# Gated attention loop: the chunk's small jobs between its two value products, the second maxima behind them, and two 8-column steps with other operands

## The chip, the cores and the metric

The kernel runs on one core of a Trainium2 chip as a single program. The metric is the device time of one execution in microseconds; the number compared is the median of several runs.

## The reference

Four layers follow each other on `x` of shape (2, 1024, 128), each as `x = x + layer(layernorm(x))`: a linear ("flow") attention layer with feed-forward part, a gated attention layer, a narrow multi-head attention layer, and a mixture of experts. The change lies in the second, which is:

```python
s = sigmoid(x @ Ws)                                   # (b, t, 8 heads)
vals, idx = top_k(s, 3)
scores = zeros_like(s).at[bi, ti, idx].set(vals)      # gates: 3 of 8 heads
q, k, v = heads(x @ Wq), heads(x @ Wkv)               # 8 heads of 64
attn = softmax(einsum('bhid,bhjd->bhij', q * 64**-0.5, k))
out = einsum('bhij,bhjd->bhid', attn, v)
proj = einsum('bhtd,hde->bhte', out, Wo) + bo
return einsum('bhte,bth->bte', proj, scores)
```

## The kernel before, in words

The gated phase works on 8 pairs of heads (2 batches of 4 pairs, `G = 2` heads in a pair), each in two halves of 512 query columns. These are `HALVES = 16` halves `n`. For each half the 1024 keys are 8 tiles of 128, taken in `CHUNKS = 4` chunks `c` of two tiles, so that the loop has 64 chunks. "Chunk (n, c)" names one. The loop stands once in the program of each engine; semaphores join them, and no engine reorders its own list.

In each chunk TensorE makes the scores of two key tiles into PSUM banks 0 to 3 (`score`, L1453 for the negative shift and L1460 for the products). ScalarE takes the exponential (`probs`, L1567). TensorE multiplies the probabilities of the chunk before with the values (`mix`, L1473, twice in a chunk, into bank 4), and GpSimd adds them up (`tally`, L1327, two instructions in most chunks) for the denominators.

The softmax needs the row maxima of a half before its scores. They are made far ahead, as "pairs": two score products (`maximum`, L1355) whose results VectorE reduces (L1671, into `maxima`). Eight pairs make a half, and two pairs go into a chunk, the first and the second maxima. After the last pair of a half VectorE merges two columns of maxima into `top` (L1676, 128x8), TensorE turns it in the job `shift` (L1368), VectorE writes `shift_t` (L1690), and SyncE carries it to the row `neg`.

Everything else is a small "job":

- `proj`: projection of a later pair of heads (L71 to L73). ScalarE copies it to `high` (L1516), VectorE subtracts to `low` (L1662).
- `den`: denominators of the half before, from `tally` (L1373); VectorE copies them to `den_rows` (L1694).
- `dent`: those rows turned back (L1378). VectorE inverts eight columns into `inv` (L1701) and multiplies them by the gates into `coef` (L1704).
- `out`, for each of the two heads: the output product (L1408, both in one stretch); VectorE adds it to `X` with `coef` (L1730, four instructions a head).
- `turn`, `bias` (halves 2 to 5, chunks 0 and 1), `gate` and its choice (half 0), and the jobs `fturn`, `fproj`, `fvalue` that prepare the next phase (halves 10 to 13; L1036, L71 to L73, L1713, L1717, L1720).

All jobs and maxima share three PSUM banks, 5 to 7, in rotation: `order` is the list of all of them, `number` a job's place in it, `bank_of(job) = JOB_BANK + number[job] % 3`. TensorE may write a bank once VectorE has used the job three places before, which it learns from the counter `job_used`. A pair waits `job_used >= number[pair[1]] - 2`, an output product `job_used >= number - 1` of its first job. VectorE walks through `order` strictly.

`between(n, c)` lists the jobs that stand behind the first maxima: in order `shift` (c = 2), `proj` (chunks 0 and 1 of even halves, 2 and 3 of odd ones), `gate`, `fturn`, `fproj`, `fvalue`, then `den` (c = 2) or `dent` (c = 3). `behind(n, c)` lists the output products (c = 3) and `turn` and `bias`. TensorE's order in a chunk is: scores, first maxima, first value product, `between`, second maxima, second value product, `behind`.

From chunk (14, 2) on there are no maxima any more. The loop ends with `den`, `dent` and `out` of the last half, and a barrier leads to the narrow attention phase.

Of the kernel before, what the change touches and what calls it, by code (L numbers as in the profile page):

```python
# [13 lines left out]
ALU = mybir.AluOpType  # L14
ACT = mybir.ActivationFunctionType
AX = mybir.AxisListType
# [4 lines left out]
P = 128  # L21
# [941 lines left out]
class Front:  # L963
# [5 lines left out]
    H, DH, G = 16, 8, 4  # L969
# [146 lines left out]
def gated_attention_phase(nc, psum, X, C, io, stale, front):  # L1116
# [5 lines left out]
    H, DH, TOPK, G = 8, 64, 3, 2  # L1122
# [5 lines left out]
    QT = BANK // P  # L1128
    STEPS = G * QT
# [5 lines left out]
    with ExitStack() as ctx:  # L1135
        ph = Phase(nc, ctx, "gated")
# [38 lines left out]
        front_U = old_values[:, PARTS:PARTS + SEQ].rearrange("p (t d) -> p t d", d=D)  # L1175
        front_UH, front_UL = UH[:, 0:SEQ], UL[:, 0:SEQ]
        front_rest = w_raw[:, 0:2 * BANK].rearrange("p (k t) -> p k t", k=2)
        inv = ph.sb("inv", [P, STEPS])
        coef = ph.sb("coef", [P, 2, STEPS])
        norm = Norm(ph, "norm", X, U)  # L1180
        shift_ready, ws_zero = ph.sem("shift_ready"), ph.sem("ws_zero")
# [58 lines left out]
        def behind(n, c):  # L1240

            now = []
            if n >= 1 and c == 3:
                now += [("out", n - 1, 0), ("out", n - 1, 1)]
            if 2 <= n < 2 + QUARTERS and c < 2:
                now.append((("turn", "bias")[c], n - 2))
            return now

        def maxima_of(n, c, e):
            i = n_lead + 2 * (n * CHUNKS + c) + e  # L1250
            return max_pair(i) if i < HALVES * MAXPAIRS else []

        tail = [("den", HALVES - 1), ("dent", HALVES - 1), ("out", HALVES - 1, 0), ("out", HALVES - 1, 1)]
        order = lead + [job for n in range(HALVES) for c in range(CHUNKS)
                        for job in maxima_of(n, c, 0) + between(n, c) + maxima_of(n, c, 1) + behind(n, c)] + tail
        number = {job: i for i, job in enumerate(order)}

        def bank_of(job):
# [73 lines left out]
        def _(pe):  # L1332
# [163 lines left out]
            for n in range(HALVES):  # L1496
                for c in range(CHUNKS):
                    i = n * CHUNKS + c
                    score(n, c)
                    for e in range(2):  # L1500
                        pair = maxima_of(n, c, e)
                        if pair:
                            maximum(pair)
                        if i >= 1:
                            mix(i - 1, e)
                        small((between, behind)[e](n, c))
            for e in range(2):
                mix(HALVES * CHUNKS - 1, e)
            small(tail)
# [81 lines left out]
        def _(dve):  # L1591
# [51 lines left out]
            for i, job in enumerate(order):  # L1643
                bank = bank_of(job)
                if job in position:
                    here = position[job]
                    if here in STATS_AT:
                        dve.wait_ge(job_used, number[("out", 6 + STATS_AT[here], 1)] + 1)
                        front.norm.quarter_stats(dve, STATS_AT[here])
                    if here == CENTER_AT:  # L1650
                        for q in range(PERB):
                            front.center(dve, q)
                    if here in LOWEST_AT:
                        front.lowest(dve, LOWEST_AT[here], front_part, front_rest)
                if job in (max_pair(6)[0], max_pair(8)[0]):
                    turned_low(2 + (job == max_pair(8)[0]))
                if job[0] == "proj":
                    _, g, m, x = job
                    parts += 1
                    cols = slice(x * BANK, (x + 1) * BANK)  # L1660
                    dve.wait_ge(high_taken, parts)
                    dve.tensor_tensor(low[:, g % 3, m, cols], psum[:, bank, :], f32(high[:, g % 3, m, cols]),  # L1662
                                      ALU.subtract).then_inc(job_used, 1)
                    continue
                dve.wait_ge(job_done, i + 1)
                if job[0] == "max":
                    _, n, j, qt, x = job
                    if n >= 2 and j == qt == x == 0:
                        dve.wait_ge(top_ready, n - 1)
                    at = j * QT + qt  # L1670
                    dve.tensor_reduce(maxima[:, n % 2, x, at:at + 1], psum[:, bank, :], AX.X, ALU.max).then_inc(job_used, 1)  # L1671
                    if (j, qt, x) == (G - 1, QT - 1, 1):
                        dve.wait_ge(job_used, i + 1)
                        if n >= 1:
                            dve.wait_ge(job_done, number[("shift", n - 1)] + 1)
                        dve.tensor_tensor(top[:, :], maxima[:, n % 2, 0, :], maxima[:, n % 2, 1, :], ALU.max).then_inc(top_ready, 1)  # L1676
                    if job in CHOICE_AT:
                        choose_step(CHOICE_AT[job])
                elif job[0] == "gate":
                    turned_gates = psum[:, bank, :].rearrange("p (i q s) -> p q i s", q=QUARTERS, s=32)[:, :, :, 0:H]  # L1680
                    by_quarter = scores[:, :, :].rearrange("p (q i) h -> p q i h", q=QUARTERS)
                    dve.tensor_scalar(by_quarter, turned_gates, 1.0, None, ALU.add).then_inc(gate_step, 1)
                    dve.wait_ge(gate_step, 1)
                    dve.reciprocal(scores[:, :, :], scores[:, :, :]).then_inc(gate_step, 1)
                    dve.sem_inc(job_used, 1)
                elif job[0] == "shift":
                    n = job[1]
                    if n >= 1:
                        dve.wait_ge(shift_loaded, 64 * n)
                    dve.tensor_scalar(shift_t[:, :], psum[0:STEPS, bank, 0:P], -1.0, None, ALU.mult).then_inc(job_used, 1)  # L1690
                    dve.wait_ge(job_used, i + 1)
                    dve.sem_inc(shift_copied, 1)
                elif job[0] == "den":
                    dve.tensor_copy(den_rows[:, :], psum[:, bank, :]).then_inc(job_used, 1)  # L1694
                elif job[0] == "dent":
                    n = job[1]
                    t0, h0 = n // 2 // PAIRS * STILES + n % 2 * QT, n // 2 % PAIRS * G
                    dve.wait_ge(job_used, i)
                    if n == 0:
                        dve.wait_ge(gate_step, 8)  # L1700
                    dve.reciprocal(inv[:, :].rearrange("p (t j) -> p t j", j=G),  # L1701
                                   psum[:, bank, :].rearrange("p (t j d) -> p t j d", j=G, d=DH)[:, :, :, 0]).then_inc(inv_ready, 1)
                    dve.wait_ge(inv_ready, n + 1)
                    dve.tensor_tensor(coef[:, n % 2, :].rearrange("p (t j) -> p t j", j=G), inv[:, :].rearrange("p (t j) -> p t j", j=G),  # L1704
                                      gates[:, t0:t0 + QT, h0:h0 + G], ALU.mult).then_inc(job_used, 1)
                elif job[0] == "turn":
                    if job[1] >= 1:
                        dve.wait_ge(job_done, number[("bias", job[1] - 1)] + 1)
                    dve.tensor_copy(gates_t[:, :], psum[0:H, bank, :]).then_inc(job_used, 1)
                elif job[0] == "fturn":  # L1710
                    front.turned_low(dve, bank, job[1], front_UH, front_UL)
                    dve.wait_ge(front.lo_turned, job[1] + 1)
                    dve.sem_inc(job_used, 1)  # L1713
                elif job[0] == "fproj":
                    front.without_high(dve, bank, job[1], front_part, front_rest)
                    dve.wait_ge(front.rest_ready, job[1] + 1)
                    dve.sem_inc(job_used, 1)  # L1717
                elif job[0] == "fvalue":
                    to, made = front.value_view(bank, job[1])
                    dve.tensor_copy(to, made).then_inc(job_used, 1)  # L1720
                elif job[0] == "bias":
                    dve.wait_ge(job_used, i)
                    part = X[:, job[1] * PER_Q:(job[1] + 1) * PER_Q, :]
                    dve.tensor_tensor(part, part, psum[:, bank, :].rearrange("p (t d) -> p t d", d=D), ALU.add).then_inc(job_used, 1)
                else:
                    _, n, j = job
                    t0 = n // 2 // PAIRS * STILES + n % 2 * QT
                    dve.wait_ge(job_used, i)
                    for t in range(QT):
                        last = dve.scalar_tensor_tensor(X[:, t0 + t, :], psum[:, bank, tile(t)],  # L1730
                                                        coef[:, n % 2, t * G + j:t * G + j + 1], X[:, t0 + t, :], ALU.mult, ALU.add)
                    last.then_inc(job_used, 1)
# [710 lines left out]
```

## Time and profile before

| | |
|---|---|
| median of 3 runs | 1275.22 us |
| lowest and highest run | 1272.82, 1278.53 us |
| profiled execution, its own time | 1267.5 us |
| its span, first to last instruction | 1265.7 us |
| gated loop, scores of (0, 0) to the last update of `X` | about 208 to 623.6 us |
| mean granted clock of TensorE | 0.934 |

The span lies inside the execution's own time. Everything that is worked out from the trace belongs to the profiled execution, so it is set against 1267.5 us and not against the median. A row of a timeline has the start, the duration (for merged instructions until the last one ends), the engine, the line, what it writes and reads, how many instructions it holds, and in brackets how long the engine was idle before it and for whom. Matmuls overlap their successors, so the time between the starts of two rows says what one costs in a busy stretch.

### The profile page before, as it was taken

To read this page: it belongs to the slowest core of one execution; us is meant where nothing else is said; L and a number is where in the kernel's file an instruction comes from. 1 tells how busy PE (TensorE), PEld (TensorE's weight loads), DVE (VectorE), ACT (ScalarE), POOL (GpSimd) and SP (SyncE) were. 2 spreads that over 40 slices of the span, in tenths; PEclk is the share of its full clock that TensorE was granted. 3 is DMA by queue.
4 is the path that set the end of the run, shared out by engine and by line. 5 is a ranking of instruction groups with operands and counts; after the bars stand their busy time and mean duration, and the time that the engine had idled before them with its cause. 6 is when DMAs were issued, how large, how long until landed. Compare 5 with 4: busy or idle time off the path is not lost. (4 is left out here: it accounts for less than half of the span.)

```text
span 1265.7 us, 18746 instructions
## 1 busy us (share of the span) xinstructions
PE 1106.5 (87%) x6921; PEld 558.3 (44%) x6921; DVE 951.1 (75%) x1606; ACT 712.1 (56%) x1207; POOL 377.9 (30%) x239
## 2 busy tenths in 40 slices
PE   4389959999999989999789999999999778999995
PEld 3256735444444444444232222222222276888884
DVE  7958488767666766675589999999998176778777
ACT  5224546333333354433327777878787727888883
POOL 1038212755767656667500000000000021112110
PEclk9569979989999999999859999999999968999998
DMA  3000010000000000001020000000000023143421
GB/s 90 1 1 3 1 34 2 10 1 1 1 2 2 2 1 1 26 18 35 15 73 18 16 24 15 26 13 27 13 2 1 1 35 77 43 84 62 76 47 33
DMA packets 46354, 29.43 MB, mean 23 GB/s; under 512 B 10992, under 2 KB 43000, under 8 KB 46264
## 3 DMA queue, kind: packets, MB, share of 16 engines
q1 hardware_dynamic: 46264, 28.24, 9.5%
q8 instruction: 55, 0.90, 0.3%
q14 instruction: 35, 0.29, 0.1%
HBM read 23.57 MB, written 4.26 MB: 22 GB/s over the span
## 5 line engine op out<-in xcount | busy, mean ns | idle before, releaser
L2032 DVE TENSOR_REDUCE narrow_att_maxima<-psum 128x1 f32<-128x1024 f32 x256 | 301.8, 1219 | 28.6 <-PE psum L1884 26.0
L1991 ACT ACTIVATE narrow_att_probs<-psum 128x512 f32<-128x512 f32 x512 | 266.4, 603 | 79.2 <-PE psum L1910 79.1
L1327 POOL TENSOR_TENSOR gated_tally<-gated_probs,gated_tally 128x1024 f32<-128x1024 f32 x96 | 230.1, 2397 | 72.5 <-ACT gated_probs L1567 64.0
L1567 ACT ACTIVATE gated_probs<-psum 128x1024 f32<-128x1024 f32 x128 | 124.3, 1022 | 202.3 <-PE psum L1460 202.3
L1671 DVE TENSOR_REDUCE gated_maxima<-psum 128x1 f32<-128x512 f32 x256 | 164.3, 683 | 59.2 <-PE psum L1355 57.3
L1910 PE MATMUL psum<-narrow_att_q,narrow_att_k 50*128 50x512 bf16 x448 | 145.4, 383 | 6.3 <-ACT narrow_att_probs L1991 5.2
L1923 PE MATMUL psum<-narrow_att_probs,narrow_att_v_ones 128*32 128x512 f32 x1024 | 137.2, 607 | 10.3 <-ACT narrow_att_sums L1981 10.2
L1884 PE MATMUL psum<-narrow_att_k,narrow_att_q 48*128 48x512 bf16 x448 | 130.3, 380 | 16.3 <-DVE narrow_att_maxima L2032 11.7
L1473 PE MATMUL psum<-gated_probs,gated_values 128*64 128x512 f32 x512 | 138.0, 619 | 0.0
L2324 DVE TENSOR_TENSOR moe_hidden_lo<-moe_hidden,moe_hidden_hi 128x512 fp32r<-128x512 f32 x144 | 100.8, 725 | 46.8 <-ACT moe_hidden_hi L2293 46.4
L2289 ACT ACTIVATE moe_hidden<-psum,moe_up_bias 128x512 f32<-128x512 f32 x144 | 96.0, 685 | 37.1 <-PE psum L73 35.9
L1884 PEld LDWEIGHTS psum<-narrow_att_k,narrow_att_q 48*128 48x128 bf16 x448 | 27.0, 94 | 137.5 <-DVE narrow_att_maxima L2032 126.1
L2293 ACT ACTIVATE moe_hidden_hi<-moe_hidden 128x512 fp32r<-128x512 f32 x144 | 86.4, 628 | 0.0
L1355 PE MATMUL psum<-gated_high 64*128 64x512 f32 x256 | 58.6, 452 | 17.5 <-DVE gated_low L1662 10.4
L1327 POOL TENSOR_TENSOR gated_tally<-gated_probs 128x1024 f32<-128x1024 f32 x16 | 37.9, 2372 | 89.7 <-ACT gated_probs L1567 89.7
L1910 PEld LDWEIGHTS psum<-narrow_att_q,narrow_att_k 50*128 50x128 bf16 x448 | 32.9, 93 | 58.2 <-ACT narrow_att_probs L1991 53.9
L1460 PE MATMUL psum<-gated_high 64*128 64x512 f32 x256 | 58.4, 451 | 0.0
L71 PE MATMUL psum<-moe_UH,moe_up_hi 128*128 128x512 f32 x144 | 58.3, 405 | 0.0
L72 PE MATMUL psum<-moe_UL,moe_up_hi 128*128 128x512 f32 x144 | 58.1, 404 | 0.0
L73 PE MATMUL psum<-moe_UH,moe_up_lo 128*128 128x512 f32 x144 | 57.6, 400 | 0.0
L71 PE MATMUL psum<-moe_hidden_hi,moe_down_hi 128*128 128x512 f32 x144 | 57.1, 396 | 0.0
L72 PE MATMUL psum<-moe_hidden_lo,moe_down_hi 128*128 128x512 f32 x144 | 57.0, 396 | 0.0
(362 smaller groups left out, 1836.5 us busy)
## 6 DMA issues: line engine op xcount, KB each, us to landing
moe_mixb<-moe_mix_scratch SPq DMA_DIRECT2D x8, 1024.0 KB, 15.9
moe_raw_up<-in_L_ffn_up_w SPq DMA_DIRECT2D x8, 256.0 KB, 16.1
moe_raw_down<-in_L_ffn_down_w SPq DMA_DIRECT2D x8, 256.0 KB, 12.1
narrow_parts_scratch<-gated_values SPq DMA_DIRECT2D x12, 128.0 KB, 2.1
narrow_parts_scratch<-narrow_att_part SPq DMA_DIRECT2D x12, 128.0 KB, 2.1
narrow_att_q<-narrow_parts_scratch SPq DMA_DIRECT2D x14, 96.0 KB
narrow_att_q<-narrow_parts_scratch SPq DMA_DIRECT2D x42, 32.0 KB
narrow_att_k<-narrow_parts_scratch SPq DMA_DIRECT2D x14, 96.0 KB
```

The lines of the kernel that those rows point to most:

```text
L71: pe.matmul(out, a_hi, b_hi, start=start, stop=False, skip_group_check=True)
L72: pe.matmul(out, a_hi, b_lo, start=False, stop=False, skip_group_check=True)
L1327: pool.tensor_tensor(tally[:, n % 2, :, :], probs[:, kt % 4, :, :], so_far, ALU.add).then_inc(tallied, 1)
L1473: last = pe.matmul(psum[DH * j:DH * j + DH, SUM_BANK, :], values[:, t, c0:c0 + DH], probs[:, kt % 4, j, :], start=(kt == 0), stop=(kt == S ...
L1567: act.activation(probs[:, k % 4, :, :], psum[:, 2 * e:2 * e + 2, :], ACT.Exp, scale=SCALE).then_inc(exped, 1)
L1671: dve.tensor_reduce(maxima[:, n % 2, x, at:at + 1], psum[:, bank, :], AX.X, ALU.max).then_inc(job_used, 1)
L1884: done = pe.matmul(psum[:, i % 2 * 2 + x, :], qs(n // 2, n % 2, r)[64 * a:64 * a + ROWS, tile(qt)], ks(n // 2, x, r)[64 * a:64 * a + ROWS, ...
L1910: pe.matmul(psum[:, SCORE_BANK + j % 3, :], ks(n // 2, kt // QT, e)[rows, tile(kt % QT)], qs(n // 2, n % 2, e)[rows, :], start=True, stop= ...
L1923: last = pe.matmul(psum[32 * j:32 * j + 32, SUM_BANK, :], v_ones[:, n // 2 % 2, kt, j, :], probs[:, (n * STILES + kt) % 3, j, :], start=(k ...
L1991: act.activation(probs[:, k % 3, 2 * e + u % 2, :], psum[:, SCORE_BANK + j % 3, :], ACT.Exp, scale=SCALE).then_inc(exped, 1)
L2032: dve.tensor_reduce(maxima[:, n % 2, column(u):column(u) + 1], chunk.rearrange("p a b -> p (a b)"), AX.X, ALU.max).then_inc(chunk_used, 1)
L2324: dve.tensor_tensor(hidden_lo[:, k % 2, a, :], hidden[:, k % 2, a, :], f32(hidden_hi[:, k % 2, a, :]), ALU.subtract).then_inc(hidden_lo_re ...
```

## The change

Three edits, all in the gated phase:

1. The order in a chunk, for all engines and on TensorE. It becomes: scores, first maxima, first value product, `between`, `behind`, second value product, second maxima. The numbers of the jobs change with it, and so the banks and waits.
2. The inverse of the denominators is written back to the PSUM columns that it was read from, `inv` is gone, and `coef` is made from `gates` in SBUF and those columns in PSUM.
3. `top` is made by one reduction over the two columns of maxima instead of an element-wise maximum of two SBUF operands.

```diff
-        inv = ph.sb("inv", [P, STEPS])
...
-                        for job in maxima_of(n, c, 0) + between(n, c) + maxima_of(n, c, 1) + behind(n, c)] + tail
+                        for job in maxima_of(n, c, 0) + between(n, c) + behind(n, c) + maxima_of(n, c, 1)] + tail
...
                     for e in range(2):
+                        if i >= 1 and e == 1:
+                            mix(i - 1, 1)
                         pair = maxima_of(n, c, e)
                         if pair:
                             maximum(pair)
-                        if i >= 1:
-                            mix(i - 1, e)
-                        small((between, behind)[e](n, c))
+                        if e == 0:
+                            if i >= 1:
+                                mix(i - 1, 0)
+                            small(between(n, c) + behind(n, c))
...
-                        dve.tensor_tensor(top[:, :], maxima[:, n % 2, 0, :], maxima[:, n % 2, 1, :], ALU.max).then_inc(top_ready, 1)
+                        dve.tensor_reduce(top[:, :], maxima[:, n % 2, :, :].rearrange("p x s -> p s x"), AX.X, ALU.max).then_inc(top_ready, 1)
...
-                    dve.reciprocal(inv[:, :].rearrange("p (t j) -> p t j", j=G),
-                                   psum[:, bank, :].rearrange("p (t j d) -> p t j d", j=G, d=DH)[:, :, :, 0]).then_inc(inv_ready, 1)
+                    turned_den = psum[:, bank, :].rearrange("p (t j d) -> p t j d", j=G, d=DH)[:, :, :, 0]
+                    dve.reciprocal(turned_den, turned_den).then_inc(inv_ready, 1)
                     dve.wait_ge(inv_ready, n + 1)
-                    dve.tensor_tensor(coef[:, n % 2, :].rearrange("p (t j) -> p t j", j=G), inv[:, :].rearrange("p (t j) -> p t j", j=G),
-                                      gates[:, t0:t0 + QT, h0:h0 + G], ALU.mult).then_inc(job_used, 1)
+                    dve.tensor_tensor(coef[:, n % 2, :].rearrange("p (t j) -> p t j", j=G), gates[:, t0:t0 + QT, h0:h0 + G],
+                                      turned_den, ALU.mult).then_inc(job_used, 1)
```

## Rows read from the trace of the kernel before

**Rows 1.** The page: busy time, share of the span, and instructions of each engine.

```profile
PE 1106.5 (87%) x6921; PEld 558.3 (44%) x6921; DVE 951.1 (75%) x1606; ACT 712.1 (56%) x1207; POOL 377.9 (30%) x239
```

**Rows 2.** The table of windows: length, busy time by engine, clock, DMA, GB/s.

```profile
210.00:610.00 400.00, 373.37 (x2261) 175.23 (x2261) 271.39 (x491) 157.66 (x190) 265.06 (x119) 0.99 0.03 8
```

**Rows 3.** The waits of TensorE's matmuls, 208 to 615 us: total, times, longest.

```profile
PE psum L1355 <- DVE gated_low L1662: 10.2, 13, 1.5
PE psum L1408 <- DVE gated_maxima L1671: 9.9, 13, 1.2
PE psum L1355 <- DVE gated_maxima L1671: 3.0, 3, 1.7
```

**Rows 4.** The timeline of TensorE in chunk (5, 3).

```profile
356.30 0.51 PE L1453 MATMUL psum<-gated_neg,gated_ones_r 1*128 1x512 f32 x4
...
358.24 0.40 PE L1355 MATMUL psum<-gated_high 64*128 64x512 f32 x2
...
360.38 0.60 PE L1378 MATMUL psum<-ident,gated_den_rows 128*128 128x128 f32 x4
361.96 0.50 PE L1355 MATMUL psum<-gated_high 64*128 64x512 f32 x2 [0.97 <-DVE gated_low L1662]
362.39 1.08 PE L1473 MATMUL psum<-gated_probs,gated_values 128*64 128x512 f32 x4
364.45 1.16 PE L1408 MATMUL psum<-gated_wo_raw,gated_sums 64*128 64x128 f32 x16 [0.98 <-DVE gated_maxima L1671]
365.54 0.51 PE L1453 MATMUL psum<-gated_neg,gated_ones_r 1*128 1x512 f32 x4
```

**Rows 5.** The timeline of VectorE in the same chunk.

```profile
361.21 0.69 DVE L1662 TENSOR_TENSOR gated_low<-psum,gated_high 128x512 fp32r<-128x512 f32 x1 [1.25 <-ACT gated_high L1516]
362.00 0.21 DVE L1701 RECIPROCAL gated_inv<-psum 128x8 f32<-128x8 f32 x1
362.25 1.50 DVE L1704 TENSOR_TENSOR gated_coef<-gated_inv,gated_gates 128x8 f32<-128x8 f32 x1
363.67 1.28 DVE L1671 TENSOR_REDUCE gated_maxima<-psum 128x1 f32<-128x512 f32 x2
365.61 2.36 DVE L1730 SCALAR_TENSOR_TENSOR X<-psum,gated_coef,X 128x128 f32<-128x128 f32 x8 [0.67 <-PE psum L1408]
```

**Rows 6.** The timeline of GpSimd in the same chunk.

```profile
358.86 4.87 POOL L1327 TENSOR_TENSOR gated_tally<-gated_probs,gated_tally 128x1024 f32<-128x1024 f32 x2 [2.23 <-ACT gated_probs L1567]
```

**Rows 7.** Lines L1676 and L1704: shortest, median, longest in ns; then one instance.

```profile
L1676 DVE TENSOR_TENSOR gated_top<-gated_maxima x16: 171/648/2349, 197.8 to 585.6; 128x8 f32<-128x8 f32 x16
...
L1704 DVE TENSOR_TENSOR gated_coef<-gated_inv,gated_gates x16: 166/1424/2364, 254.2 to 620.4; 128x8 f32<-128x8 f32 x16
...
620.36 0.17 DVE L1704 TENSOR_TENSOR gated_coef<-gated_inv,gated_gates 128x8 f32<-128x8 f32 x1
```

**Rows 8.** The timeline of TensorE, second maxima of chunk (5, 2).

```profile
354.86 0.50 PE L1355 MATMUL psum<-gated_high 64*128 64x512 f32 x2 [0.40 <-DVE gated_low L1662]
```

**Rows 9.** The timeline of TensorE, in chunks (0, 2) and (6, 3).

```profile
223.91 0.50 PE L1355 MATMUL psum<-gated_high 64*128 64x512 f32 x2 [1.70 <-DVE gated_maxima L1671]
...
388.34 1.16 PE L1408 MATMUL psum<-gated_wo_raw,gated_sums 64*128 64x128 f32 x16 [0.27 <-DVE gated_maxima L1671]
```

**Rows 10.** The timeline of TensorE in the last half and behind it.

```profile
601.91 1.94 PE L1473 MATMUL psum<-gated_probs,gated_values 128*64 128x512 f32 x8
...
603.77 0.51 PE L1453 MATMUL psum<-gated_neg,gated_ones_r 1*128 1x512 f32 x4
...
617.50 1.08 PE L1373 MATMUL psum<-gated_tally,gated_ones 128*64 128x512 f32 x4 [1.30 <-POOL gated_tally L1327]
```

**Rows 11.** The table of windows around the clock, and an output product of half 1.

```profile
208.00:270.00 62.00, 57.06 (x315) 26.97 (x315) 45.67 (x69) 24.11 (x28) 38.94 (x16) 0.92 0.02 5
270.00:620.00 350.00, 326.14 (x2012) 152.68 (x2010) 232.56 (x436) 137.33 (x166) 233.18 (x106) 1.00 0.03 8
625.00:670.00 45.00, 36.70 (x111) 13.47 (x113) 38.45 (x52) 16.45 (x32) 1.59 (x4) 0.51 0.20 64
...
256.45 1.95 PE L1408 MATMUL psum<-gated_wo_raw,gated_sums 64*128 64x128 f32 x16 [0.98 <-DVE gated_maxima L1671]
```

## The prediction

> **What bounds the kernel now.** I read the page first, for the shares of the engines and the slices: TensorE is busy 87% of the 1265.7 us span and VectorE 75% [rows 1]. The change touches only the gated attention loop, so the next view is the table of windows for 210 to 610 us, where almost all of its 64 chunks run. There TensorE is busy 373.4 of 400 us, VectorE 271.4, ScalarE 157.7 and GpSimd 265.1 [rows 2]. TensorE is the bound, and what an order can give back is at most its idle time, 400.0 - 373.4 = 26.6 us. The table of waits, for TensorE alone, splits that into kinds [rows 3]: 13 waits of the output product (L1408) for a maximum, 9.9 us; 13 of a maxima product (L1355) for `low`, 10.2 us; 3 of one for other maxima, 3.0 us; the rest, 3.5 us, are maxima products waiting for other projection-like jobs.
>
> The timeline of one fourth chunk of an odd half shows both large kinds [rows 4]. The chunk starts with its scores at 356.30. First maxima at 358.24, value product, projection, `dent` at 360.38. The second maxima could follow at 360.99 but start at 361.96, 0.97 us idle, because the bank needs the projection's `low`, which VectorE ends at 361.90 [rows 5]. Then the value product at 362.39, and the output product waits 0.98 us until 364.45: it needs the bank of the first of the second maxima, whose reduction begins only at 363.67 [rows 5]. What is in front of it on VectorE is the 8-element coefficient, 1.50 us long. It ends at 363.75, just as GpSimd's two tallies, begun at 358.86, end at 363.73 [rows 6]. The same instruction takes 0.17 us when GpSimd is idle; over its 16 instances it runs from 0.166 to 2.364 us, and `top` from 0.171 to 2.349 [rows 7]. So a 0.2 us instruction waits out a GpSimd instruction, and TensorE pays for it two steps later.
>
> **The change part by part.**
>
> *Coefficient.* `inv` leaves SBUF, so the coefficient reads one operand in PSUM and one in SBUF. `low`, of exactly that kind on 512 columns, takes 0.69 us with the tallies running [rows 5]. I take the coefficient at its unheld 0.17 us plus at most 0.1; the bounds are 0.17 and today's 1.50. The in-place reciprocal stays at its 0.21 [rows 5], since it read PSUM already and only its output moves; it cannot cost much more than the 0.25 between the starts of reciprocal and coefficient. The Trainium skill (SBUF — State Buffer, "Who interferes with whom") says that a VectorE instruction with two SBUF inputs shares a read port with GpSimd and may wait out its whole instruction, and one with a single SBUF input does not. The end times here agree to 0.02 us, and by that rule the hold is gone; without it, the first rival below holds.
>
> *Top.* A reduction with a single input of 16 elements; nearest is the same step unheld, 0.17 us, and above it the 512-element reduction, 0.68. Either way it is off the path. For the next half `top` is made at the end of the second chunk and used by the `shift` transpose behind 3.3 us of scores, maxima and value product in the third. Maxima (0.43 + 1.29) and 0.2 end 1.9 us after the pair starts, 1.7 us early. Value: 0. If it stayed held it would still be hidden, since GpSimd's pair ends before the shift.
>
> *Order, third chunk with projection* (halves 1, 3, 5, 7, 9 to 12; den follows). The second maxima wait for `low` by 0.40 to 0.93 us (one of them in [rows 8]). The second value product, 1.01 us [rows 4], now stands in front of them and covers all of it. These eight waits are 4.0 us of the list in rows 3 (the ones of 0.4 to 0.5 us and one of 0.93). Gain 4.0.
>
> *Order, fourth chunk with projection* (halves 1, 3, 5, 7, 9 to 13, nine of them). The output product takes the place of the second maxima behind `dent`. It needs the same bank in rotation and so waits for the same `low`: 0.97 us stays. It starts at 361.96 - 356.30 = 5.66 us into the chunk. The value product follows (1.09 + 1.01), free at 5.66 + 2.10 = 7.76. The second maxima now need the bank of the *first* output product, so four of the eight `X` updates: they start 365.61 - 364.45 = 1.16 us after the output product [rows 4, 5], four take 2.36 / 2 = 1.18, and 0.06 for the semaphore (as 361.90 to 361.96) makes 2.40. The pair waits 0.30 us, starts at 8.06, and takes 0.43. Chunk: 8.49 instead of 365.54 - 356.30 = 9.24, gain 0.75. VectorE must be free at 5.66 + 1.16 = 6.82: `low`, reciprocal and coefficient end at about 6.1 if unheld. If held, at 363.75 - 356.30 = 7.45, and the chunk is 0.7 longer again.
>
> *Order, fourth chunk without projection* (halves 2, 4, 6, 8). The 0.27 us wait of the output product for maxima goes [rows 9], the 0.30 for `X` comes: 0.
>
> *Other maxima waits.* The 1.70 us at 223.91 [rows 9] and those of the chunks (9,0) and (13,0), 0.92 and 0.33, have up to 1.01 us of cover each. VectorE is full around 224 with the gate's choice, so part returns later: of 3.0 us I take 2.2.
>
> *Adjacent value products.* In chunks with no job between them the two products now run as one group. In the loop's last, short chunks two of them take 603.77 - 601.91 = 1.86 us [rows 10], against 2 x 1.01. That is 0.15 less in some ten chunks: 1.5 us.
>
> As a sum over kinds: 9.9 (output products) + 4.0 + 2.2 + 1.5 - 13 x 0.30 = 13.7 us. The last chunks are unaffected: the last `den` waits for GpSimd's last tally [rows 10], and those tallies start from the scores of the last half, which move up with everything. The job banks and ScalarE's order stay. Nothing in the DMA queues moves except with the shift, whose neg rows have three chunks of time.
>
> **Later pairs, a check.** Behind a fourth chunk VectorE ends `X` 3.52 us after the output product started, 9.18 into the chunk, then the first of the second maxima at 9.9. The next chunk's first maxima come at 8.49 + 1.94 = 10.4 and need it. 0.5 us of slack remains.
>
> **The clock.** TensorE's granted clock over 208 to 270 us is 0.92, and 1.00 from 270 to 620 [rows 11]: 0.08 x 62 x 2 = 10 us at the low of the two levels (1.2 against 2.4 GHz). At the low level the output product took 1.95 us against 1.16 [rows 4, 11]. The stretches came right behind the 1.70 us wait and behind the waits of 0.97 and 0.98 of half 1. About half of 10 us is lost, 5 us. The same waits in later halves left the clock alone, so I count nothing for it and keep 5 us both ways in the range. Behind the loop 45 us have a clock of 0.51, through a barrier that the change leaves as it is.
>
> **Rivals.**
> 1. *The hold stays* on the coefficient, because its other operand or GpSimd's timing is what matters. Nine chunks cost 0.7 us more: 13.7 - 6.3 = 7.4, so 1268. For: only ends coincide. Against: `low` with one SBUF operand is never long. 0.13.
> 2. *The clock comes too.* Fewer waits in halves 0 and 1 keep the high level: 13.7 + 5 = 18.7, so 1256.5. The Trainium skill (TensorE: Matmul & The Clock Gate, "HAM oscillation — how this bites in real kernels") has gaps in TensorE's work as what throttles it. The waits before both stretches agree with it, the nine later ones do not. 0.17.
> 3. *No difference.* The second maxima wait for all eight `X` updates, or the 0.5 us of slack is not there and the pair of the next chunk waits as well: 1.18 us in each of 13 fourth chunks is 15.3 us, and the time is 1275 +- 3. Against: the wait is counted one short of the pair, so one output product is enough. 0.11.
> 4. *Slower.* The moved gaps bring the low clock back and it stays, as it does for 45 us behind the loop. One microsecond at the low level costs up to half a microsecond; to lose 13.7 and 6.4 more needs some 40 us of it inside the loop, and the place is the stalled output products, now right behind the 0.97 us gap. At 45 us: 1275.2 - 13.7 + 22 = 1284. For: such a stretch exists. Against: 350 us with the present gaps had none. 0.05.
>
> **How the numbers follow.** The profiled execution took 1267.5 us (span 1265.7), the median of the runs is 1275.2. The sum, 1267.5 - 13.7 = 1253.8, is made against the former; I carry the same 13.7 over to the median: 1261.5, chance 0.54. Its own range is 1258 to 1265 (the choice stretch and adjacency at nothing or double, +-3 us spread of the runs). Together the cases reach from 1253 (rival 2 with the spread) to 1271 (rival 1 with the spread), which leaves out rivals 3 and 4. 0.5% is 6.4 us, about what a measurement of this kernel can tell from no change. Faster by more: the forecast, rival 2 and most of rival 1: 0.80. Same: rival 3 and the rest of rival 1: 0.15. Slower: rival 4: 0.05.
>
> **What would show it.** In the changed profile the coefficient should be at 0.17 to 0.3 us in all 16 instances and `top` near 0.2. The waits of output products for maxima should be gone and about 13 waits of maxima products for `X` of 0.3 us be there, with some 9 waits of output products for `low` of about 1 us. Fourth chunks with projection should be 8.5 us long, third ones 6.9 instead of 7.3, and the loop's last tally should end some 14 us earlier. If the coefficient is still 1.5 us, rival 1 is right. If `X` waits are 1.5 us, rival 3. The prediction is also wrong if the stages behind the loop differ by more than the loop does.

## The result and the profile after

The changed kernel takes 1246.76 us (median of 4 runs, 1244.83 to 1247.79) against 1276.88 us before (4 runs, 1272.82 to 1280.62). The ratio is 0.9763, with a 95% interval of 0.9728 to 0.9798. That is 30 us where 13.7 were forecast, below the range. The profiled execution took 1244.83 us, 22.7 less than the 1267.5 of the one before. So there are two amounts to explain: 22.7 us between the two profiles, and 7.4 us more between the medians. The median of the kernel before is itself unsteady: in the runs of the experiments it is 1271.6 (23 runs), 1268.68 (17) and 1276.72 us (11) on three chips, so the 30 us hold for the runs compared here and not to the microsecond.

The page gives the busy times, and the table of windows the loop (the columns are those of [rows 1, 2]):

```profile
PE 1095.5 (88%) x6921; PEld 555.0 (45%) x6921; DVE 920.2 (74%) x1606; ACT 711.2 (57%) x1207; POOL 377.5 (30%) x239
```

```profile
208.00:600.00 392.00, 375.68 (x2341) 180.02 (x2341) 248.44 (x507) 161.01 (x193) 271.95 (x121) 1.00 0.03 8
```

The last chunk's scores start 379.4 us after the first chunk's (208 to 587.2), against 400.6 us before (608.5): 21.3 us of the 22.7 lie in the loop. The granted clock reads 1.00 over the whole loop; before it was 0.92 up to 270 us [rows 11]. The rest, 1.4 us, lies behind the loop: from the last chunk's scores to the end of the span it is 657.2 us before and 655.8 after.

TensorE's waits from 205 to 590 us, as in [rows 3]:

```profile
PE psum L1407 <- DVE gated_low L1664: 6.6, 6, 1.5
PE psum L1354 <- DVE X L1732: 2.4, 13, 0.2
PE psum L1354 <- DVE gated_maxima L1673: 1.2, 2, 0.6
PE psum L1407 <- DVEq L1715: 1.2, 1, 1.2
PE psum L1407 <- DVEq L1719: 1.1, 1, 1.1
PE psum L1354 <- DVE gated_low L1664: 0.9, 1, 0.9
PE psum L1407 <- DVE front_values L1722: 0.4, 1, 0.4
```

The 9.9 us of output products waiting for maxima are gone. The output products now wait for `low` (or the job in its place) nine times, and the second maxima thirteen times for `X`, 0.2 us each. All sum to 13.8 us, where there were 26.6.

The timeline of TensorE from the third to the end of the fourth chunk of half 5, the chunks of [rows 4, 8]:

```profile
345.30 1.08 PE L1372 MATMUL psum<-gated_tally,gated_ones 128*64 128x512 f32 x4
346.21 1.03 PE L1472 MATMUL psum<-gated_probs,gated_values 128*64 128x512 f32 x4
347.17 0.50 PE L1354 MATMUL psum<-gated_high 64*128 64x512 f32 x2
347.60 0.50 PE L1452 MATMUL psum<-gated_neg,gated_ones_r 1*128 1x512 f32 x4
...
353.29 1.16 PE L1407 MATMUL psum<-gated_wo_raw,gated_sums 64*128 64x128 f32 x16 [1.02 <-DVE gated_low L1664]
354.38 1.08 PE L1472 MATMUL psum<-gated_probs,gated_values 128*64 128x512 f32 x4
355.64 0.50 PE L1354 MATMUL psum<-gated_high 64*128 64x512 f32 x2 [0.17 <-DVE X L1732]
356.07 0.51 PE L1452 MATMUL psum<-gated_neg,gated_ones_r 1*128 1x512 f32 x4
```

The fourth chunk runs from 347.60 to 356.07, 8.47 us; the hand schedule gave 8.49. The output product starts 5.69 us into it (5.66), the pair 8.04 (8.06). VectorE and the two 8-column steps:

```profile
352.50 0.69 DVE L1664 TENSOR_TENSOR gated_low<-psum,gated_high 128x512 fp32r<-128x512 f32 x1 [1.26 <-ACT gated_high L1518]
353.29 0.22 DVE L1704 RECIPROCAL psum<-psum 128x8 f32<-128x8 f32 x1
353.54 0.16 DVE L1706 TENSOR_TENSOR gated_coef<-gated_gates,psum 128x8 f32<-128x8 f32 x1
354.45 2.36 DVE L1732 SCALAR_TENSOR_TENSOR X<-psum,gated_coef,X 128x128 f32<-128x128 f32 x8 [0.75 <-PE psum L1407]
```

```profile
L1678 DVE TENSOR_REDUCE gated_top<-gated_maxima x16: 169/170/173, 197.8 to 565.3; 128x8 f32<-128x16 f32 x16
...
L1706 DVE TENSOR_TENSOR gated_coef<-gated_gates,psum x16: 161/161/164, 251.2 to 599.0; 128x8 f32<-128x8 f32 x16
```

Shortest, median and longest are within 4 ns of each other, where [rows 7] had 166 to 2364 and 171 to 2349 ns. In 27 of the 32 instances a tally of GpSimd is running when they start. This is the rule of the Trainium skill (SBUF — State Buffer, "Who interferes with whom"), and the trace agrees in all 27: no second SBUF input, no wait for GpSimd.

### The profile page after: what moved, and what is told of

It reads as the page before. It is cut to its first block and busy times, and to the rows that moved or that the text cites. A ratio compares the mean times of both kernels' runs of the same rounds, so it can differ in the third digit from the quotient of the medians.

```text
span 1243.0 us, 18745 instructions
## 1 busy us (share of the span) xinstructions
PE 1095.5 (88%) x6921; PEld 555.0 (45%) x6921; DVE 920.2 (74%) x1606; ACT 711.2 (57%) x1207; POOL 377.5 (30%) x239
## 5 line engine op out<-in xcount | busy, mean ns | idle before, releaser
L1925 PE MATMUL psum<-narrow_att_probs,narrow_att_v_ones 128*32 128x512 f32 x1024 | 137.2, 608 | 10.3 <-ACT narrow_att_sums L1983 10.2
L1472 PE MATMUL psum<-gated_probs,gated_values 128*64 128x512 f32 x512 | 134.0, 612 | 0.0
```

What stands on the lines that cost most here:

```text
L1472: last = pe.matmul(psum[DH * j:DH * j + DH, SUM_BANK, :], values[:, t, c0:c0 + DH], probs[:, kt % 4, j, :], start=(kt == 0), stop=(kt == S ...
L1925: last = pe.matmul(psum[32 * j:32 * j + 32, SUM_BANK, :], v_ones[:, n // 2 % 2, kt, j, :], probs[:, (n * STILES + kt) % 3, j, :], start=(k ...
```

## The experiments

Loop length below is the time from the scores of chunk (0, 0) to those of (15, 3) in the run's profile: 400.6 us before, 379.4 changed. Chunk lengths are between the starts of their first score matmuls.

**The kernel before, again.** No edit.

> The kernel before once more, unchanged, to see how its runs differ from its first profile, which at 1267.5 us was 9.4 us under the median of the four runs. Theory 1 (the clock): the other runs spend more of the loop at TensorE's low clock level, so the mean granted clock of the runs is lower than 0.934 where the time is longer, about 0.007 for 9 us more. Rival (chip or memory): the time differs at the same mean clock, by longer transfers or barriers. Time 1272 to 1281 us, ratio 1.000.

The ratio is 0.9993 (0.9955 to 1.0031). The 12 runs spread from 1263.59 us at a mean granted clock of 0.936 to 1280.93 at 0.921, and 23 runs of the kernel before on the same chip from 1263.49 (0.937) to 1281.68 (0.921), and where the clock of one run is lower than that of another by 0.003 or more, its time is longer. The clock tells the time: 0.016 of some 1270 us is 2 x 0.016 x 1270 = 41 us more at the low level and 18.2 us more time, 0.45 us for each. In the profile the low level comes at other places than in [rows 11], and the timeline shows where:

```profile
500.00:560.00 60.00, 55.16 (x297) 26.24 (x296) 37.72 (x69) 22.65 (x28) 32.71 (x15) 0.89 0.04 14
```

```profile
514.22 0.50 PE L1355 MATMUL psum<-gated_high 64*128 64x512 f32 x2 [0.98 <-DVE gated_low L1662]
516.70 1.89 PE L1408 MATMUL psum<-gated_wo_raw,gated_sums 64*128 64x128 f32 x16 [0.97 <-DVE gated_maxima L1671]
518.52 0.80 PE L1453 MATMUL psum<-gated_neg,gated_ones_r 1*128 1x512 f32 x4
```

The waits of 0.98 and 0.97 us of chunk (11, 3), then the output product at half speed, as in half 1 of the first profile. Chunk (11, 3) and its successor take 9.97 and 7.95 us instead of 9.23 and 5.60, 3.1 us together, and (12, 3) and its successor are held up in the same way. The nine fourth chunks with projection are places where that can happen. In the three profiles of kernels with both waits (the first, this one and that of top alone, below) the low level comes behind 6 of their 27, at five different ones of the nine, and at other ones in each profile but for (12, 3), which has it twice. Theory 1 holds on the clock; the median of 1270.7 us is a little below the 1272 to 1281 that were expected.

Not all of the spread lies in the loop. This profile's span is 4.5 us longer than the first one's (1270.2 and 1265.7), and of that the loop has 1.8 (402.4 and 400.6 us) and the stretch behind it 2.7 (659.9 and 657.2). There too the granted clock is lower, here first in the profile of rows 1 to 11, then in this one:

```profile
990.00:1062.00 72.00, 55.13 (x279) 39.09 (x280) 38.24 (x107) 36.55 (x67) 7.83 (x10) 0.76 0.15 26
990.00:1062.00 72.00, 53.34 (x271) 35.48 (x264) 37.60 (x104) 35.76 (x65) 7.72 (x10) 0.74 0.12 21
```

The mean clock of a timed run therefore says how much time it spent at the low level, and not where.

**Order alone.**

```diff
# the order of the changed kernel; inv, coef and top as before
-  maxima_of(n, c, 0) + between(n, c) + maxima_of(n, c, 1) + behind(n, c)
+  maxima_of(n, c, 0) + between(n, c) + behind(n, c) + maxima_of(n, c, 1)
```

> Only the order of the chunk is changed; coefficient and top keep two SBUF operands. My hand schedule: with the coefficient held until GpSimd's pair ends, a fourth chunk with projection is 9.1 to 9.2 us (8.47 in the changed kernel, 9.24 before), third ones about 6.5 to 6.9, and the loop is 10 to 12 us shorter at the same clock, ratio 0.991. If order also removes the low clock in halves 0 to 2 it is 14 to 16 us in the profile. Rival (order does it all, the hold was hidden): 17 us at the same clock and fourth chunks of 8.5 us.

Ratio 0.987 (0.9816 to 0.9925), median 1254.17 us. Loop 386.5 us in the profile, 14.1 less; without what the low level had cost there before (3.9 us, below) 10.2. The fourth chunks with projection take 9.14 us:

```profile
355.53 1.16 PE L1408 MATMUL psum<-gated_wo_raw,gated_sums 64*128 64x128 f32 x16 [1.02 <-DVE gated_low L1665]
356.62 1.08 PE L1473 MATMUL psum<-gated_probs,gated_values 128*64 128x512 f32 x4
358.54 0.50 PE L1355 MATMUL psum<-gated_high 64*128 64x512 f32 x2 [0.84 <-DVE X L1733]
```

```profile
355.77 1.49 DVE L1707 TENSOR_TENSOR gated_coef<-gated_inv,gated_gates 128x8 f32<-128x8 f32 x1
357.36 2.10 DVE L1733 SCALAR_TENSOR_TENSOR X<-psum,gated_coef,X 128x128 f32<-128x128 f32 x7
```

The held coefficient makes the `X` updates late and the wait of the second maxima 0.84 us instead of 0.17. The first reading holds; the rival, that the order does it all, falls. Two of the six runs stand at 1260.2 and 1261.0 us with a clock of 0.929 and 0.928, the other four at 1252.7 to 1254.3 with 0.936 and more. Two waits near a microsecond are still in each of those chunks, and the low level still comes in some executions; that it comes behind these waits is likely and not shown, since the profile, with none of it in the loop, fell on one of the four.

**Coefficient alone.**

```diff
# order and top as before
+                    turned_den = psum[:, bank, :].rearrange(...)[:, :, :, 0]
+                    dve.reciprocal(turned_den, turned_den).then_inc(inv_ready, 1)
+                    dve.tensor_tensor(coef[...], gates[...], turned_den, ALU.mult).then_inc(job_used, 1)
```

> Only the coefficient is changed (PSUM and SBUF operand), order and top as before. Theory: the coefficient takes 0.16 us everywhere, the output products wait no more for maxima: 0.98 us in nine fourth chunks and 0.28 in four, about 9.9 us of the loop, ratio 0.992, and fourth chunks with projection are 8.3 us. Rival: the wait moves to another job and the gain is under 4 us. If the low clock in halves 0 to 2 hangs on the wait in front of the output product of half 1, its stretch there goes too and the profile shows 3 us more.

Ratio 0.9872 (0.9812 to 0.9932), median 1254.75 us; loop 386.8 us. The output product follows the value product at once:

```profile
356.95 0.50 PE L1355 MATMUL psum<-gated_high 64*128 64x512 f32 x2 [0.98 <-DVE gated_low L1662]
357.38 1.08 PE L1473 MATMUL psum<-gated_probs,gated_values 128*64 128x512 f32 x4
358.39 1.16 PE L1408 MATMUL psum<-gated_wo_raw,gated_sums 64*128 64x128 f32 x16
```

Fourth chunks with projection take 8.17 us and those without 6.40 (6.73): 9 x 1.06 + 4 x 0.33 = 10.9 us at an equal clock, where 9.9 was expected. So this edit alone is worth as much as the order alone. The two share the wait of the output products, so that together they give 16.3 us (the run with both and without `top`, below), not 21. The stretch at the low level in half 1 is gone, as expected if it hangs on that wait, but the second profile of the kernel before lacks it too, so this proves nothing. Two of the six runs stand at 1262.47 and 1256.96 us with 0.929 and 0.930, although of the two waits only the 0.98 in front of the pair is left, with the 1.7 us of chunk (0, 2).

**Top alone.**

```diff
# order and coefficient as before
-  dve.tensor_tensor(top[:, :], maxima[:, n % 2, 0, :], maxima[:, n % 2, 1, :], ALU.max)
+  dve.tensor_reduce(top[:, :], maxima[:, n % 2, :, :].rearrange("p x s -> p s x"), AX.X, ALU.max)
```

> Only top is changed to a reduction. As predicted it is worth nothing: ratio 1.000, waits of output products unchanged at 9.9 us. Rival: the 2.35 us hold delays the maxima in front of projection in third chunks (7.31 us before, 6.48 after the change, where the 0.40 us wait alone explains half), then third chunks with projection shrink by some 0.2 us, 1.8 us in all, ratio 0.9985.

Ratio 1.0005 (0.9967 to 1.0044): nothing that the times can tell. The chunks tell a little: third chunks of halves 1, 7 and 13 are 0.23, 0.21 and 0.14 us shorter, the others keep their length. Its profile has four stretches of 6.8 us at the low level in the loop, behind fourth chunks 3, 10 and 12 and in half 0, and took 1277.15 us.

**The waits filled.**

```diff
# the kernel before; filler(n, c, k) waits exped >= 2 * i + 2, then writes k pairs of score products
# (64x512, start and stop set) to banks 0 to 3, which the next chunk's scores overwrite
+                        if e == 1 and stalled:            # fourth chunks with projection
+                            filler(n, c, 4)
+                        if e == 1 and (n, c) == (0, 2):
+                            filler(n, c, 6)
                         if pair:
                             maximum(pair)
                         if i >= 1:
                             mix(i - 1, e)
+                        if e == 1 and stalled:
+                            filler(n, c, 4)
```

> The kernel before with TensorE kept busy in its waits: in the nine fourth chunks with projection four pairs of surplus score products, written to the score banks after the exponentials have been read, in front of the second maxima and again in front of the output products, and six such pairs in chunk (0, 2). The results are not used and are overwritten. They take 0.23 us a pair, as long as the waits they stand in, so at an equal clock the loop keeps its length (0 to 3 us longer). Theory (gaps throttle): no stretch at the low clock level remains between 208 and 600 us, runs of one kernel lie within 5 us, median 1262 to 1266, ratio 0.994. Rival (the dips come by themselves, or by heavy work): stretches stay in the loop, runs spread over 15 us as before, ratio 1.000 to 1.003.

The surplus products are the only difference to the kernel before, and they are in the place of the two waits:

```profile
358.19 1.21 PE L1484 MATMUL psum<-gated_high 64*128 64x512 f32 x8
359.24 0.50 PE L1355 MATMUL psum<-gated_high 64*128 64x512 f32 x2
359.67 1.08 PE L1473 MATMUL psum<-gated_probs,gated_values 128*64 128x512 f32 x4
360.68 1.19 PE L1484 MATMUL psum<-gated_high 64*128 64x512 f32 x8
361.73 1.16 PE L1408 MATMUL psum<-gated_wo_raw,gated_sums 64*128 64x128 f32 x16
```

```profile
208.00:606.00 398.00, 389.52 (x2426) 186.82 (x2424) 272.79 (x494) 159.48 (x192) 263.36 (x118) 1.00 0.03 8
```

The chunk keeps its 9.24 us, 353.58 to 362.82, and the loop has no stretch at the low level; it is 397.4 us long, 3.2 less than before. Of its 12 runs eleven lie between 1264.33 and 1269.21 and one at 1274.03 (0.927). Of the 17 runs of the kernel before on the same chip, seven lie above 1272, five of them at 1280 to 1281 with 0.920 or 0.921. The ratio is 0.9957 (0.9925 to 0.999). More work and less time: in the loop it is the gaps that bring the low level. The gain is small all the same. The median, 1266.67 us, is just above the 1262 to 1266 that were expected, and the profiled execution as a whole, 1268.7 us with a span of 1265.8, is no shorter than the first one of the kernel before (1265.7): the 3.2 us of the loop are lost again, 1.0 ahead of it and 2.3 behind it, where the surplus products change nothing. The spread was to shrink to 5 us; it did but for one run, so a rest of the dips has another place or survives.

**Order and coefficient, top as before.**

```diff
# the changed kernel with
+  dve.tensor_tensor(top[:, :], maxima[:, n % 2, 0, :], maxima[:, n % 2, 1, :], ALU.max)
```

> The change without its third edit: top is held by GpSimd again. By my prediction top is worth nothing and this equals the changed kernel, 1246.8 us. By the runs with order alone, where third chunks of halves 1, 7 and 13 are 0.33, 0.35 and 0.27 us longer than in the changed kernel, it is 1 us slower, 1248; fourth chunks 8.47 us.

Ratio 0.9807 (0.9759 to 0.9856), median 1248.3 us, loop 380.5 us against 379.4. Fourth chunks are 8.47, third ones of halves 1, 7 and 13 are 0.31, 0.34 and 0.27 us longer than in the changed kernel. The timelines of VectorE and TensorE in chunk (7, 2) show the way:

```profile
391.30 1.49 DVE L1679 TENSOR_TENSOR gated_top<-gated_maxima 128x8 f32<-128x8 f32 x1
392.71 1.27 DVE L1674 TENSOR_REDUCE gated_maxima<-psum 128x1 f32<-128x512 f32 x2
```

```profile
393.16 0.27 PE L1368 MATMUL psum<-ident,gated_top 128*8 128x128 f32 x1
393.54 0.47 PE L71 MATMUL psum<-gated_UH,gated_wqk_hi 128*128 128x512 f32 x1
```

The first maxima are queued behind the held `top`, and the projection, which needs their bank, starts 0.38 us after the `shift`. Unheld it starts 0.03 us after it (344.39 and 344.42 in the changed kernel's chunk (5, 2)). Top is worth 1.1 us of the loop, not nothing.

**Projection behind the output products.**

```diff
# between(n, c) of the changed kernel; behind(n, c) without the output products
+            if n >= 1 and c == 2:
+                now.append(("den", n - 1))
+            if n >= 1 and c == 3:
+                now = [("dent", n - 1), ("out", n - 1, 0), ("out", n - 1, 1)] + now
```

> The changed kernel with dent and both output products in front of projection, fturn, fproj and fvalue in fourth chunks, so that the output products wait for no low. By the hand schedule the output products start 3.87 us into the chunk, the second maxima wait for all eight updates of X until 7.4 and the chunk is 7.9 us instead of 8.47: 9 times 0.55, about 5 us, ratio to before 0.973, some 5 us under the changed kernel. Rival: low ends later on VectorE and holds the next chunk's maxima, then nothing is gained.

Ratio 0.975 (0.9699 to 0.9802), median 1241.46 us. The output product starts 3.86 us into the chunk and the nine chunks take 7.87 to 7.91 us:

```profile
346.74 0.50 PE L1452 MATMUL psum<-gated_neg,gated_ones_r 1*128 1x512 f32 x4
...
350.60 1.16 PE L1407 MATMUL psum<-gated_wo_raw,gated_sums 64*128 64x128 f32 x16
...
354.21 0.50 PE L1354 MATMUL psum<-gated_high 64*128 64x512 f32 x2 [0.55 <-DVE X L1732]
354.65 0.51 PE L1452 MATMUL psum<-gated_neg,gated_ones_r 1*128 1x512 f32 x4
```

The loop is 373.9 us, 5.5 less than the changed kernel's. The schedule is right, and the later `low` holds nobody in the loop. Behind the loop the profile is 1.5 us longer (657.3 and 655.8), so the profiled execution gains 3.7 us.

**The pair and the value product exchanged, and nothing else of the order.**

```diff
# the changed kernel, behind(n, c) back at the end of the chunk in order and on TensorE
-                            small(between(n, c) + behind(n, c))
+                            small(between(n, c))
+                        else:
+                            small(behind(n, c))
```

> The changed kernel with the jobs of behind back at the end of the chunk; only the second maxima and the second value product have changed places. Tells what the move of the output products is worth. Hand schedule: fourth chunks with projection 8.35 us (8.47 in the changed kernel), without projection 7.1 (6.65), so 1 us slower or equal in the loop, 1246 to 1249 us. Rival (moving the jobs is what gives the 17 us): fourth chunks of 9 us and a loop 5 us longer or more.

Ratio 0.9797 (0.9749 to 0.9844), median 1246.95 us. Loop 377.8 us, 1.6 *less* than the changed kernel. Fourth chunks with projection are 0.40 us shorter (8.05 to 8.07 us for 8.47 in five of them, 8.35 expected) except the last, (13, 3), which is 0.22 longer; those without take 7.28 (6.65). `turn` and `bias` at the chunk's end save 0.38 to 0.55 us in four chunks, 1.9 in all, of which other chunks give 0.8 back. In sum -3.0, +2.5 and -1.1 us. So moving the output products between the value products gives nothing over all; putting the pair behind the value product is what covers `low`. The expectation had the right two effects and the wrong sign of their sum.

**The changed kernel and the late projection, on one chip.** No new edit in either.

> The changed kernel once more, beside the version with the late projection on the same chip. If the low clock level in the loop is what made the kernel before run from 1263 to 1281 us, the changed kernel, whose only longer gaps are the 1.02 us waits of the output products, stays within 5 us: 1244 to 1249, ratio 0.98 and clock 0.935 or more in all runs.

> The version with dent and output products ahead of projection in fourth chunks, once more: 5 us under the changed kernel of the same call (9 fourth chunks of 7.89 instead of 8.47 us), 1240 to 1242 us, and no stretch at the low level in the loop.

The changed kernel: 1247.1 us, six runs of 1245.14 to 1248.78, clock 0.932 to 0.939 (one run below the 0.935 that was expected of all), ratio 0.9781 (0.9747 to 0.9816). The late projection: 1242.02, five runs of 1241.0 to 1242.93 and one of 1250.28 at 0.925, ratio 0.975 (0.9714 to 0.9785). The two intervals overlap and hang on the same runs of before. The medians differ by 5.1 us, the loops by 5.6 (373.9 and 379.5), and only the run at 1250.28 lies above the fastest of the other. The kernel before, on the same chip, had 11 runs from 1269.26 (0.932) to 1280.6, its median 1276.72 at 0.928.

## Why the prediction was wrong, and where it was right

**The direction, the cause and the fourth chunks were right.** The coefficient was held by GpSimd, it is not any more, and at the chunks in which that told the schedule was right to 0.02 us. Nine fourth chunks give 6.8 us, and 9 x 0.75 = 6.75 is what their step says. (The sum over kinds had 9.9 - 3.9 = 6.0 for them and the four others; measured are 6.8 + 0.3. The waits for `X` are 0.17 to 0.21 us on TensorE, not 0.30.) Plain chunks with adjacent value products gave 1.4, where 1.5 was said. The other maxima waits gave 2.7 (2.2).

**The step that failed is the clock**, "so I count nothing for it and keep 5 us both ways", together with carrying 13.7 over from the profiled execution to the median. The forecast was short by 16.4 us (30.1 and 13.7). Of these 3.7 are sizes at an equal clock, 3.9 the low level in the loop of the profile, 1.4 lie behind the loop, and 7.4 are the step from the profiles to the medians. The profiled execution before was one of the lighter draws: 10 us at the low level in the loop, behind two places. With (0, 3), (1, 3) and (2, 0) at the lengths of the second profile of the same kernel (5.45, 9.23, 6.17 us), they had cost 0.8 + 0.8 + 2.3 = 3.9 us. That, the 17.4 us of the loop at an equal clock and the 1.4 behind it make the 22.7 between the profiles.

The median run before had more. In the last set of runs it is 1276.72 us at a clock of 0.928, against 1245.47 at 0.939 in the changed kernel's profile: 2 x 0.011 x 1270 = 28 us at the low level, and at 0.45 us each 12.6 us. With the 17.4 that makes 30.0 of the 31.3 between these two. From median to median the clocks are 0.928 and 0.935 to 0.936, which gives 8 to 9 us by the same price and 26 of the 29.6. So the clock's share of the medians is an estimate of 9 to 12 us, a few us are left over, and where the low level lay in the timed runs no profile shows; part of it can be behind the loop.

The argument against rival 2, that nine later waits had left the clock alone, took one execution for all. The second and the top profile have the low level behind the fourth chunks of other halves, and the filled kernel shows that in the loop it goes with the gaps. The Trainium skill (TensorE: Matmul & The Clock Gate, "HAM oscillation — how this bites in real kernels") has gaps in TensorE's work as what throttles it. On this the runs agree, but the page's own case has waits of several microseconds, and here waits of 0.97 us are enough in some executions.

**A size that was off: third chunks.** 4.0 us were forecast, 6.5 measured. I priced them by TensorE's idle time alone, 0.40 us in [rows 8]. The timeline after has 0.91 us from `den` to the value product and 0.96 from it to the pair; before, `den` to the pair of [rows 8] took 1.49 with 0.40 idle, so 1.09, and the value product 1.01:

```profile
353.37 1.08 PE L1373 MATMUL psum<-gated_tally,gated_ones 128*64 128x512 f32 x4
```

`den` with a value product of its own shape right behind it costs 0.18 less, and the value product in front of the pair 0.05 less: 0.63 us a chunk. The same effect had been counted for plain chunks and missed here; why products of one shape are cheaper side by side, no run shows. Another 0.2 in halves 1 and 7 is that of `top`, which the text put at nothing: it looked whether `shift` waits, and not at who is queued behind `top` on VectorE. In halves 3 and 5 the other 0.2 comes from `bias`, which no longer stands directly in front of these chunks' scores: scores to first maxima take 1.94 us, and 2.14 before. On the whole it is no gain, as (3, 1) and (5, 1) are 0.4 longer.

| at an equal clock, us | forecast | measured |
|---|---|---|
| fourth chunks, all 13 | 6.0 | 7.1 |
| third chunks with projection, eight | 4.0 | 6.5 |
| chunks (0, 2), (0, 3), (9, 0), (13, 0) | 2.2 | 2.7 |
| adjacent value products | 1.5 | 1.4 |
| all others (`turn` and `bias` -0.7, (13, 2) +0.3) | 0 | -0.3 |
| loop, sum of these | 13.7 | 17.4 |
| low clock level in the loop, profile | 0 | 3.9 |
| behind the loop, profile | 0 | 1.4 |
| low clock level anywhere, median run (estimate) | 0 | 9 to 12 |

Rival 1 (the hold stays) falls with the 161 ns. Rival 3 (the pair waits for all updates) falls with 0.17 us. Rival 4 (the low level stays in the loop) was the wrong way round. Rival 2 was right in kind; its 5 us fit the 3.9 of the profile and are about half of what the median run lost. What stays open is why an execution drops the clock at one fourth chunk and not at the next, and the single runs at 1274, 1262 and 1250 us of kernels without the pair of gaps (filled, coefficient alone, late projection). No profile fell on one of these.

## What to carry to other kernels

Before a profile's sum is carried to a median, ask whether the profile was a typical draw: the mean granted clock of each run tells it at once, and pairs of waits of a microsecond on a nearly full TensorE are a lottery ticket each. Removing such a pair is then worth its length and its share of the low clock; here the second came to an estimated 9 to 12 us beside 17.4 at an equal clock. A single wait need not go for that: the changed kernel keeps one of about 1.02 us or more in eight fourth chunks, and both of its profiles have the whole loop at the high level. For an in-order vector engine, price a held instruction by everything that stands behind it, and look for one that reads two SBUF operands while GpSimd works: an 8-column step can cost what a 1024-column one does.

## What had not been expected of the hardware

- The same program, on one chip, takes 1263.5 to 1281.7 us, and the mean granted clock (0.937 to 0.921) orders the runs. Each microsecond at the low level costs 0.45 us here over the whole program, and 3.9 / 10.2 = 0.38 in the loop of the first profile.
- Two waits of 0.97 us, 2.5 us apart in a stretch where TensorE is otherwise full, are followed by 6.8 us at the low level in 6 of 27 places of three profiles and by nothing in the others. With useless products in them the loop had none of it and was 3.2 us shorter than in the first profile.
- Two dense float32 products of 512 columns behind each other take 1.86 us as value products, and `den` in front of one 0.91 instead of 1.09.
- A reduction from SBUF of 16 elements (170 ns) and a product of PSUM and SBUF operands (161 ns) are never held by GpSimd's tallies. The in-place reciprocal in PSUM costs 0.217 us against 0.208 with its output in SBUF.
